# Small attentions on one core: VectorE's order within a unit, with normalising and residual first and the values at the end of the second unit

## The reference, cut to what matters

```
scores = einsum('bhqd,bhkd->bhqk', q, k) / sqrt(16)       # q, k, v: linear maps of 256 channels
scores = scores * mask + (what the mask takes away)
probs  = softmax(scores, axis=-1)
out    = einsum('bhqk,bhkd->bhqd', probs, v)
x      = x + out @ w_o + b_o
```

## Time and profile before

| what | value |
|---|---|
| median of 3 runs | 1951.75 us (1951.03 to 1952.35) |
| the profiled execution | 1954.09 us |
| its span, first to last instruction | 1952.3 us |
| mean granted TensorE clock, share of full speed | 0.982 |
| PE busy | 1857.6 us, 95% of the span |
| DVE busy | 1105.9 us, 57% |
| ACT busy | 1042.2 us, 53% |
| POOL busy | 998.7 us, 51% |

### The profile page before, as it was taken

One profiled execution on the slowest core, in us unless ns is written; L12 is line 12 of the kernel. 1 busy time (PEld: TensorE's weight loads), 2 busy tenths in 40 slices (PEclk: granted clock), 3 DMA queues, 4 the chain that ended last, 5 costly groups with the idle time before them and its releaser, 6 DMA issues.

```text
span 1952.3 us, 37701 instructions
## 1 busy us (share of the span) xinstructions
PE 1857.6 (95%) x14320; PEld 1502.8 (77%) x14320; DVE 1105.9 (57%) x2104; ACT 1042.2 (53%) x1945; POOL 998.7 (51%) x1140
## 2 busy tenths in 40 slices
PE   7999989989996999999999999999999998999999
PEld 5776779534454788888888888888888887966788
DVE  3656556489999555454544544544444445746554
ACT  4555543434344655665655656656665654345532
POOL 6766742366754544654544544544454535357620
PEclk9999999989998999999999999999999999999999
DMA  6000010000001222322322322322322310010000
GB/s 239 2 2 2 2 58 1 1 1 1 1 1 38 76 82 90 95 82 82 108 82 82 109 82 82 105 86 82 108 82 82 106 47 1 22 44 2 2 12 33
DMA packets 61841, 108.01 MB, mean 55 GB/s; under 512 B 7008, under 2 KB 42336, under 8 KB 60256
## 3 DMA queue, kind: packets, MB, share of 16 engines
q1 hardware_dynamic: 60784, 103.38, 17.0%
q10 hardware_dynamic: 880, 2.22, 0.3%
HBM read 103.47 MB, written 2.10 MB: 54 GB/s over the span
## 4 chain that ended last, share of the span: by engine, by line
PE 81%; DVE 9%; issue 4%; POOL 3%; ACT 2%; DMA 0%; DVEq 0%; SPq 0%; ACTq 0%; POOLq 0%
PE banks L864 18%; PE banks L935 9%; PE banks L892 9%; PE banks L629 7%; PE banks L471 7%; PE banks L646 6%; PE banks L924 6%; PE banks L905 3%; PE banks L528 2%; PE banks L553 2%; PE banks L480 2%; PE banks L510 2%; PE banks L465 2%; PE banks L913 1%; PE banks L539 1%
## 5 line engine op out<-in xcount | busy, mean ns | idle before, releaser
L1985 POOL TENSOR_TENSOR w_lo<-w2ring,w_hi 128x512 fp32r<-128x512 f32 x128 | 180.5, 1410 | 244.7 <-ACT w_hi L1130 244.7
L1807 DVE TENSOR_REDUCE nmax<-banks 128x4 f32<-128x260 f32 x128 | 54.2, 424 | 308.8 <-PE banks L905 308.8
L2068 POOL TENSOR_TENSOR wo_lo<-wo_ring,wo_hi 128x256 fp32r<-128x256 f32 x128 | 93.3, 738 | 250.5 <-ACT wo_hi L1338 250.4
L1795 DVE TENSOR_TENSOR v<-banks,dbv 128x512 f32<-128x512 f32 x128 | 88.6, 692 | 158.6 <-PE banks L892 158.5
L1338 ACT ACTIVATE wo_hi<-wo_ring 128x256 fp32r<-128x256 f32 x128 | 53.1, 417 | 190.3 <-PE banks L935 189.5
L935 PE MATMUL banks<-wo_hi,c_hi 128*128 128x256 f32 x512 | 148.8, 291 | 4.4 <-DVE c_lo L1800 4.4
L935 PE MATMUL banks<-wo_lo,c_hi 128*128 128x256 f32 x512 | 146.1, 285 | 0.0
L935 PE MATMUL banks<-wo_hi,c_lo 128*128 128x256 f32 x512 | 146.0, 285 | 0.0
L1325 ACT ACTIVATE k<-banks,cols 128x512 f32<-128x512 f32 x128 | 88.2, 689 | 80.4 <-PE banks L864 80.4
L924 PE MATMUL banks<-PT,v 128*128 128x128 f32 x1024 | 124.7, 275 | 1.0 <-issue 0.8
L924 PEld LDWEIGHTS banks<-PT,v 128*128 128x128 f32 x1024 | 119.7, 192 | 1.6 <-issue 1.2
(11 more groups left out here) (235 smaller groups left out, 5468.3 us busy)
## 6 DMA issues: line engine op xcount, KB each, us to landing
w2ring<-in_w SPq DMA_DIRECT2D x128, 384.0 KB, 3.1
b2ring<-in_b SPq DMA_DIRECT2D x128, 128.0 KB, 4.0
wo_ring<-in_wo SPq DMA_DIRECT2D x128, 128.0 KB, 3.3
mlp_w<-in_mlp SPq DMA_DIRECT2D x6, 1024.0 KB, 6.9
wl<-in_wres SPq DMA_DIRECT2D x1, 2688.0 KB, 9.0
X<-in_x_in SPq DMA_DIRECT2D x4, 512.0 KB, 11.1
wb<-in_wres SPq DMA_DIRECT2D x2, 1024.0 KB, 11.4
ctxT<-in_ctx_in SPq DMA_DIRECT2D x4, 512.0 KB, 19.4
```

The source lines that it names most:

```text
L1795: V.tensor_tensor(v2[i], held(("v2", v, i)).rearrange("p (s d) -> p s d", s=HV), dbv, ALU.add).then_inc(S["l2_v"], 1)
L1985: G.tensor_tensor(w2_lo[:, n % 2, :], w2ring[:, n % HR, 0:2 * KT * P], w2_hi[:, n % 2, :].bitcast(f32), ALU.subtract).then_inc(S["l2_wlo"], 1)
L2068: G.tensor_tensor(wo_lo[:, n % 2, :], wo_ring[:, n % WR, :], wo_hi[:, n % 2, :].bitcast(f32), ALU.subtract).then_inc(S["l2_wolo"], 1)
```

## The change

Only DVE's order within a unit is changed. Before, a unit was `scale(n)`; at p = 2 `values(ai, 0)`; `largest(n - 1)`; at p = 2 `values(ai, 1)`; `weighed(n - 4)`; at p = 3 `update(ai - 2)`; then `split` or `stats`. Now `weighed(n - 4)` and `update` stand first, then `scale(n)` and `largest(n - 1)`, and both halves of `values` stand at the end of p = 1 instead of around `largest` of p = 2. `split` and `stats` keep their place at the end. No instruction is added or taken away on any engine; the semaphores waited for are the same.

```diff
                         it = attended(ai)
-                        scale(n)
-                        if p == 2:
-                            if ai - 2 >= start:
-                                dve.wait_ge(S["att_pv"], UNITS * (ai - 1))
-                            values(ai, 0)
-                        if n > UNITS * start:
-                            largest(n - 1)
-                        if p == 2:
-                            values(ai, 1)
                         if n - LAG - 1 >= UNITS * start:
                             weighed(n - LAG - 1)
                         if p == 3 and ai - 2 >= start:
                             update(attended(ai - 2))
+                        scale(n)
+                        if n > UNITS * start:
+                            largest(n - 1)
+                        if p == 1:
+                            if ai - 2 >= start:
+                                dve.wait_ge(S["att_pv"], UNITS * (ai - 1))
+                            for g in range(2):
+                                values(ai, g)
                         if p == 2 and ai + 1 == stop:
                             split(it + 1)
```

## The result

| | median | range | runs |
|---|---|---|---|
| before, on the same chip | 1952.35 us | 1951.03 to 1952.60 | 5 |
| changed | 1942.87 us | 1937.86 to 1946.16 | 5 |
| the forecast | 1933.8 us | 1929.5 to 1941.2 | |

The ratio is 0.9945, with a 95% interval of 0.9926 to 0.9963. The change is faster by 9.5 us where 17.9 were forecast, and its median lies outside the forecast range. The runs of the change spread over 8.3 us, these five of before over 1.6. The profiled execution of the change is its slowest: 1946.16 us, span 1944.4, mean granted clock 0.982, against the 1954.09, 1952.3 and 0.982 of before. So the two traces differ by 7.9 us.

A forecast was written before the change was run, and what follows sets the result against it. PE, busy for 95% of the span, was taken as the bound, standing still for DVE's values and residual. The terms 8.2 + 7.3 + 1.8 + 0.6 = 17.9 us, off the median 1951.75, gave 1933.8 us; range 1929.5 to 1941.2.

The forecast's parts named there:

- Part 1: Values earlier, at p = 2: PE's wait for vbd goes, 1.03 us in each of eight units, 8.2 us.
- Part 2: Residual earlier, at p = 3: PE's wait for X goes, 1.21 us in each of six units, 7.3 us.
- Part 3: Normalising earlier, all units: the 1.64 us wait for a_tok in the last group goes, plus 0.2; 1.8 us.
- What that costs: Part 2's price at p = 3: `scale` 0.88 us later, `exp` ending 0.13 before ACT is wanted, so cost zero.
- (a): Rival: at p = 3 another wait ends last, so Part 2's 7.3 us is lost; time 1941.1; chance 0.15.
- (c): Rival, slower: at p = 3 ACT's chain holds PE, 1.91 us longer in eight units; 1967.0 us; chance 0.03.
- (d): Rival: the awaited banks are not those of values and residual, so the time stays at 1951.7; chance 0.03.
- Part 4: Group ends gain 0.3 us each in two groups, 0.6; first chunk's later `scale` taken as 0, else costs 0.4 once.
- check (6): Sign looked for in the new trace: DVE's busy time is the same.
- Rival (b): Clock: moved PE gaps may remove or add lower-clock stretches; 3.4 us for two, to 1930.4 or 1937.2; chance 0.13.

The follow-up runs named there:

- r4_first_only: Only normalising and residual moved to the front, values left around the maximum of p = 2, against the kernel before: 1949.45 us, ratio 0.9973.
- the second (1952.63 - 1940.89): The changed kernel run once more, unedited, against the kernel before: 1940.89 us, ratio 0.9936.

## Where the prediction held and where it failed

**Right, by row.** Part 1: 1.03 us at each of eight p = 2, and no wait for vbd. Part 2: 1.28 instead of 1.21 at each of six p = 3; 7.7 instead of 7.3. The second way of sizing it in the prediction, 1.26 from the projections' own spacing, was the better one. Part 3: the 1.64 us are gone, and PE gains 1.9 + 0.2 = 2.1 there against 1.8. Together 18.0, forecast 17.3. "What that costs" held to the tenth, as timelines of DVE and ACT show:

```profile
148.22 1.22 DVE L1513 SCALAR_TENSOR_TENSOR T<-banks,m_pair 128x1024 f32<-128x1024 f32 x1
...
153.76 1.06 ACT L1043 ACTIVATE T<-T 128x1024 f32<-128x1024 f32 x1 [1.20 <-POOL T L1914]
154.99 1.02 ACT L1047 ACTIVATE PTs<-banks 128x1024 f32<-128x1024 f32 x1 [0.17 <-PE banks L539]
```

`scale` starts 148.22 - 146.28 = 1.94 after PE's scores (2.04 in the new order by the forecast), and ACT idled 0.17 between `exp` and the copy (0.13 by the forecast). So rivals (a), (c) and (d) did not come about. The beginning held too: PE's wait before the scores of the first p = 3 grew from 1.44 to 1.82 us, the 0.4 of Part 4, and the wait at the next unit's fell from 0.78 to 0.46, so that it cost nothing.

**The step that failed: Part 4.** It gave the ends +0.6 us; they lose 5.1. It saw that the values, 2 x 1.41 us, would leave from in front of the last unit's `scale`, and counted their going as a gain. It did not follow `split`, which stands between. Its casts moved forward, from beside POOL's two short subtractions (w_lo, 1.59 us together) to beside `masked` and `lowered` (2.34 and 2.08), and each cast lasted until 0.3 us behind the end of the POOL instruction that it met. The 2.8 us won were paid back by casts and subtractions 3.3 us longer (4.15 + 2.35 against 1.91 + 1.28).

The residual and the normalising, 1.9 us that Part 2 had moved in front of `scale` and priced for a middle chunk alone, came on top; at an end PE has no projections that would cover them. `r4_first_only` shows this part by itself: 1.8 lost at each end. The prediction had the units in hand: its rival (c) counts eight with a residual, Part 2 prices six, and the two left over are these last chunks. The rows to warn were in the trace of before: its casts in this place took 1.04 and 0.95 against 0.42 elsewhere. The prediction's check (6), "DVE's busy time is the same", was the one that caught it: it is 7.1 us more.

**Rival (b), the clock, mis-sized.** It was named with its mechanism and up to 3.4 us, and given 0.13 as a case of its own. It is not one case but goes with every run: the two profiled executions of the same program differ by 5.5 us, which stand in the row "everything else" and are the clock's but for some tenths at the start, and the 11 runs of the change by 8.3. The prediction weighed the clock by the 1.3 us between three runs of before. That was too few: over its 46 runs above the kernel before spreads over 10.7 us. So the width is not something that the change brought, and no trace of a run at 1961 us was kept that would tell what makes them long. "Such a stretch may vanish or one may come" held; for how many, one trace of before had no row.

**The account.** 17.9 forecast, +0.7 for parts 1 to 3, -5.7 for the ends (from +0.6 to -5.1): 12.9 by the schedule. Measured are 9.5 by the medians of the first comparison and 11.7 by those of the second (1952.63 - 1940.89). The 1 to 3 us between are ascribed to the clock; that is what remains, not something that a run has isolated.

**Open.** Why a wait of 1.11 us lets the clock fall in one execution and not in another of the same program was not settled. In the three traces with the fall the first scores start at 20.0 to 20.2 us; in the six without it and without filling they start at 19.2, 19.4, 20.5, 20.7 and twice 20.9. So the position in time may decide; the change was not run with its start shifted. The Trainium skill ("TensorE: Matmul & The Clock Gate", Part 1) says that the chip's window runs freely, not from the kernel's start, which would fit; no run here tests it.

## What to carry to other kernels

When an instruction moves, also look at everything that moves up behind it, up to the end of the loop, and ask what POOL is doing at the new time: here DVE's casts kept their 0.4 us beside busy PE and ACT, and its casts and its subtractions of two SBUF tiles did not keep theirs beside POOL. Price a reordering once for the steady loop and once for each first and last round, where the work that covers a step is missing. And take the range from the stretches of lower clock that can come and go, not from the spread of three runs: this kernel's second group of times, 9 us higher, did not show in its first five runs.

## What was not expected of the hardware

- A DVE cast of 128x512 took 0.42 us alone, 0.95 to 1.04 beside short POOL steps and 2.11 beside long ones; a subtraction of two SBUF tiles 0.68, and 1.2 beside POOL. The POOL instructions lost less: `lowered` 2.08 instead of 1.90, w_lo 1.02 instead of 0.72.
- The same cast took 0.57 on ACT, undisturbed by POOL. For the casts of `split` in these places that is faster than DVE.
- One program ran its second chunk once at full and once at half clock behind the same wait of 1.11 us, for 1.6 us of difference.
